# GpSimd waits for its own row transfers before every ninth one, in the sort and in the message steps of a graph network

## What is computed

```python
h = relu(layernorm(x))
edge_mats = (edge_attr @ W_bond + b_bond).reshape(-1, 32, 32)      # one 32x32 matrix an edge
for _ in range(4):                                                 # four message steps
    msg = einsum('eij,ej->ei', edge_mats, h[dst])                  # row gather by edge
    agg = segment_sum(msg, src, num_segments=12500)                # sum by the other end
    h = gru_cell(agg, h, ...)
x = x + h
h = relu(layernorm(x))
norm = deg_inv_sqrt[src] * edge_weight * deg_inv_sqrt[dst]
out = x + segment_sum(h[src] * norm[:, None], dst, 12500)
```

## Time and profile before

| | us |
|---|---|
| Time, median of 3 runs | 32566.4 (32561.8 to 32571.98) |
| Profiled execution, its own time | 32329.01 |
| Its span, first to last instruction | 32327.5 |
| Before the sort's scatters | 577.2 |
| Sort, first to last scatter | 6128.5 |
| Steps, first to last gather | 20044.9 |
| After the last gather | 5490.0 |
| GpSimd busy | 19193.7 (59%) |
| PE matmul busy | 18113.4 (56%) |
| DVE busy | 12316.8 (38%) |

### The profile page before, as it was taken

One profiled execution on the slowest core, in us unless ns is written; L12 is line 12 of the kernel. 1 busy time (PEld: TensorE's weight loads), 2 busy tenths in 40 slices (PEclk: granted clock), 3 DMA queues, 4 the chain that ended last, 5 costly groups with the idle time before them and its releaser, 6 DMA issues. The chain is left out here.

```text
span 32327.5 us, 272049 instructions
## 1 busy us (share of the span) xinstructions
PE 18113.4 (56%) x73252; PEld 11303.4 (35%) x73253; DVE 12316.8 (38%) x18995; ACT 6342.0 (20%) x11838; POOL 19193.7 (59%) x19883
## 2 busy tenths in 40 slices
PE   5444444447777757777767777775777773000004
PEld 4222222224444434444434444443444442000003
DVE  7555555533333333333333333333333333111113
ACT  4222222212222212222212222221222221000000
POOL 2444444466666656666656666665666665777772
PEclk5666666678888878888878888887888886555555
DMA  2222222211111111111111111111111111222224
GB/s 87 81 77 77 81 77 77 81 35 29 29 29 29 29 25 29 29 29 28 29 26 27 29 29 29 30 28 25 29 29 30 30 29 36 55 55 55 55 55 123
DMA packets 2423090, 1449.76 MB, mean 45 GB/s; under 512 B 1772221, under 2 KB 2253002, under 8 KB 2404167
## 3 DMA queue, kind: packets, MB, share of 16 engines
q1 hardware_dynamic: 720484, 980.18, 10.0%
q0 software_dynamic: 635936, 335.84, 6.4%
q10 hardware_dynamic: 1066560, 132.51, 2.7%
HBM read 1035.83 MB, written 411.12 MB: 45 GB/s over the span
## 5 line engine op out<-in xcount | busy, mean ns | idle before, releaser
L1112 POOL DMA_INDIRECT h_rows<-h_table,rec x12928 | 12195.4, 943 | 7353.8 <-issue 3880.5
L1298 PE MATMUL outer<-a_masked,h_by_quarter 128*128 128x272 f32 x25856 | 8240.2, 447 | 5227.6 <-DVE h_by_quarter L1158 2359.8
L1298 PEld LDWEIGHTS outer<-a_masked,h_by_quarter 128*128 128x128 f32 x25856 | 5378.2, 216 | 9576.1 <-issue 7355.3
L1266 PE MATMUL msg_psum<-outer_sums,w_bond_blocks 128*128 128x512 f32 x13736 | 7718.0, 652 | 0.0
L1344 ACT COPY outer_sums<-outer 128x544 f32<-128x544 f32 x6464 | 3900.2, 613 | 15272.9 <-PE outer L1298 7098.1
L865 POOL DMA_INDIRECT edges_by_node<-row,place x3125 | 2992.3, 958 | 3188.2 <-DVE row L792 2273.2
L1598 POOL DMA_INDIRECT messages_by_bucket<-ms,ix x3232 | 3418.9, 1058 | 1149.1 <-issue 1124.9
L1150 DVE TENSOR_TENSOR a_masked<-rec,gates 128x4352 f32<-128x4352 f32 x808 | 3782.5, 4681 | 53.1 <-PE outer L1298 31.5
L1266 PEld LDWEIGHTS msg_psum<-outer_sums,w_bond_blocks 128*128 128x128 f32 x13736 | 2921.0, 213 | 923.6 <-issue 260.9
L1167 DVE TENSOR_TENSOR_SCAN scan<-carry_flags,scan,msg_psum 128x512 f32<-128x512 f32 x404 | 517.1, 1280 | 6706.2 <-PE msg_psum L1266 4495.5
L1158 DVE TENSOR_TENSOR h_by_quarter<-h_rows,gates 128x2048 f32<-128x2048 f32 x808 | 1846.0, 2285 | 1824.4 <-DMA h_rows<-h_table,rec 1786.2
(11 more groups left out here) (273 smaller groups left out, 12928.5 us busy)
## 6 DMA issues: line engine op xcount, KB each, us to landing
h_rows<-h_table,rec POOLq DMA_INDIRECT x12928
key_row<-source_keys SPq DMA_DIRECT2D x125, 1600.0 KB
rec<-edges_by_node SPq DMA_DIRECT2D x1010, 168.0 KB
carry_flags<-carry_flags SPq DMA_DIRECT2D x505, 256.0 KB
chunk_sums<-scan_t ACTq DMA_DIRECT2D x1616, 64.0 KB
low_key_row<-source_low_keys SPq DMA_DIRECT2D x126, 800.0 KB
mr<-messages_by_bucket SPq DMA_DIRECT2D x220, 392.0 KB, 3.0
messages_by_bucket<-zeros SPq DMA_DIRECT2D x125, 689.5 KB
```

Source lines behind the costliest of these rows:

```text
L1112: pool.indirect_dma_start(out=hb[r][:, u, :], out_offset=None, in_=ht, in_offset=bass.IndirectOffsetOnAxis(ap=rec[r][:, u, W_DST:W_DST + 1 ...
L1266: last = pe.matmul(pm[:, 0:GW], wb[:, k, :], ts[b][:, k, :], start=(k == 0), stop=(k == K1 - 1))
L1298: last = pe.matmul(pt[g % RING][:, u, 0:KC], hq[j][:, g * GPB + u, :, :].rearrange("p q d -> p (q d)"), am[j][:, g * GPB + u, :, :].rearra ...
```

## The change

In the sort, GpSimd stops in front of scatters 8 and 16 (counted from 0) of each iteration until all earlier scatters of that iteration have landed. In the steps, it stops in front of gather 0 of a tile until the 16 gathers of the tile before have landed, and in front of gather 8 until gathers 0 to 7 have. Its wait for PE in front of gather 10 goes; the one in front of gather 0 stays. Nothing is computed otherwise.

```diff
@@ scatter, sort
                         for u in range(J1):
+                            if u in (8, 16):
+                                pool.wait_ge(s_sc[b], i * (16 * J1) + 16 * u)
+                                hold(pool)
                             pool.indirect_dma_start(
@@ steps
-            LATER = HALF + 2
@@ group, steps, GpSimd
                                 for u in range(J3):
-                                    if u in (0, LATER) and past:
-                                        pool.wait_ge(s_t, n0 * NB + (j * NB + NB + (HALF // GPB if u else 0)))
+                                    if u == 0 and past:
+                                        pool.wait_ge(s_t, n0 * NB + (j * NB + NB))
+                                        hold(pool)
+                                    if u == 0 and (j or past):
+                                        other = b * GI if j else (1 - b) * GI + GI - 1
+                                        pool.wait_ge(s_hg[other], (s * USES[b if j else 1 - b] + i) * (16 * J3) + (16 * J3 if j or b else 0))
+                                        hold(pool)
+                                    if u == HALF:
+                                        pool.wait_ge(s_hg[r], (s * USES[b] + i) * (16 * J3) + 16 * u)
                                         hold(pool)
                                     pool.indirect_dma_start(
```

## The result

The changed kernel takes 31,719.7 us (median of 4 runs, 31,685 to 31,774) against 32,569.2 us before (4 runs), a ratio of 0.974 with a 95% interval of 0.9724 to 0.9757. Predicted were 31,145 us. It lies in the range and on the forecast side, but 575 us above the forecast, and close to rival A's 31,770 us. Its profiled execution took 31,727.1 us, in the midst of the others: there is no gap between profile and median like the 237 us of before.

The account below looks back on a forecast made before the run. Late PE signals behind unbroken runs of about nine or more indirect DMAs bound sort and steps. Profiled 32,329 - 1500 (sort) + 80 (steps) = 30,909 us; with 237 us from profile to median, 31,145 us. Range 30,700 to 31,950 us.

Parts of the forecast that it names:

- rival A: Sort: the run of 17 scatters stays, most iterations take 42 us; 875 us gained, 80 lost, 31,770 us; chance 0.12.
- The bound: Sort and steps: unbroken runs of about nine or more indirect DMAs delay PE's signals until GpSimd pauses.
- A stop's cost: GpSimd's gap at a stop: 2.25 us for gathers, 2.15 for scatters, in place of 0.30; bounds 1.5 and above 3.68.
- Sort, GpSimd's floor of 35.6 us: Sort: GpSimd's scatters 31.6 us, two stops adding 3.7, passage to the next iteration 0.3: 35.6 us an iteration.
- Sort, 37.0 us an iteration: Sort: mean iteration 37.0 us instead of 49.0, gaining 1500 us over 125 iterations; bounds 35.6 and 41 us.
- the alternation: Sort: a run of 17 scatters makes iterations alternate between 35.6 us and 36 to 42 us.
- Steps, 23.94 us a tile: Steps: GpSimd's tile with two stops takes 23.94 us against 23.84, +80 us; bounds -320 to +640 us.
- the slack: Steps: PE is done at 43.3 us, gather 0 of tile n+2 is due at 47.8: 4.5 us of slack.
- The sum: Whole kernel: 32329 - 1500 + 80 = 30909 us profiled; with the 237 us between profile and median, 31,145 us, 4.4% less.
- B: Rival: lateness follows the number of DMAs, stops clear nothing; sort +460 us, steps +2600 us, together 35,600 us; chance 0.09.
- C: Rival: a stop of 2.0 us and a sort at GpSimd's floor; 1675 + 320 us gained, 30,570 us; chance 0.06.
- D: Rival: nothing happens in sort and steps, as the waits might be met when reached; the prediction rejected it.

## Why the prediction was right, and where it was off

*The bound* was read rightly. Late signals of PE beside unbroken runs hold back the sort; breaking the runs gives 1190 us.

*A stop's cost:* 2.15 us for a scatter against 1.97 us measured, 2.25 for a gather against 2.2. The two parts put together were right where nothing else moves data.

*Sort, GpSimd's floor of 35.6 us:* right. It is seen as 35.3 us with pauses by work.

*Sort, 37.0 us an iteration:* this term is 3.0 us too low, 375 us. The step that failed is that PE's signals "start to be late about 10 us after the run of scatters began, at its ninth": runs of eight and nine were taken as free, and only one of 17 as harmful. In the changed kernel the run of nine delays by 7.5 us a signal that PE gave 5.45 us after the run began, and a run of eight delays by 5.9 us one given after 4.1 us; the two runs of eight carry 1450 of the 2288 us of lateness. The trace of before had it already: of 79 results that PE finished during a run's sixth row, 56 were copied over 1 us late. So no iteration is free, GpSimd hardly ever gets ahead, only one run of 17 forms, and the alternation does not come. Where it came, with pauses by work, its long iteration was 57 us, not 42.

*Steps, 23.94 us a tile:* 0.52 us too low, 420 us (the forecast of +80 us became +330 against a usual execution of the old steps). The term that was mis-sized is the stop, taken at 2.25 us everywhere. In front of the second tile of a group it is 3.09 us, where the landing meets the load of `carry_flags`; in front of a first tile it is 2.19 and in front of gather 8 it is 2.20. That makes (3.09 + 2.19) / 2 + 2.20 = 4.84 us a tile instead of 4.50. The other 0.18 us stand in front of gather 1: its gap is 0.53 us in the mean, 0.23 over the usual 0.30, and not the 0.05 that was added for it. That a wait for a landing can also wait for what moves beside it was missing. The rest held: GpSimd hardly waits for PE (5.5 us in all), the slack was there, and the wait in front of gather 10 is worth nothing.

*The sum.* Carrying over the 237 us between profile and runs was wrong in kind. They lay in the two stages that the change touches, and the changed kernel's profile and median agree within 8 us. So the miss is made of three parts: 375 us in the sort, 420 in the steps, less the 237 that were added without reason, is 558 of 575 us; the stretch behind the last gather is 20 us longer than before. That the 237 us went the right way is luck: without them the miss would have been over 800 us.

*The signs.* Two of the prediction's own signs of being wrong came: gaps of 3 us and more, and late signals within runs of eight. ACT's "remote" waits for `next_free` were to fall under 1000 us and fell to 2284.7, and GpSimd's idle time in front of a first scatter was to be often under 1 us and was 5.4. In the steps most of the signs came, the stops of 2.2 us in part. So the time came near by a part of the mechanism, not by all of it.

*The rivals.* A's time came out, by another mechanism and other terms: only one run of 17 stays, iterations take 40.0 us and not 42, and the steps lose 330 us and not 80. B, that a stop clears nothing, was wrong for stops of 2 us, and right for a pause of 1.1 us, where the steps lost even more than B had it (27.85 us a tile against 27.1). Its "stops of more than 3.0 us" happened too, but only at 139 of the 804 stops in front of a gather 0. C and D fell. The rule of the Trainium skill named in the prediction, to wait for a DMA late ("DMA: Bandwidth & Descriptors", Rules for kernel authors), agrees with the steps: the waits laid open cost 330 us there. In the sort breaking the run was worth more.

## What to carry to other kernels

When waits are marked "remote" and end within about 2 us of the end of a run of GpSimd's indirect DMAs, try breaking the run before looking at the sender. Here breaks of about 2 us after every eight were enough in the steps, where breaks of 1.1 us did not help, and took away about a quarter of the sort's late waits. The break need not be a wait: GpSimd's own work does as well, and where a bulk load of another queue meets the landing it is the shorter of the two. And where the profiled execution and the median differ by more than the runs do among themselves, find the stage that varies before adding the difference to a forecast.

## What the runs showed that was not expected

- A pause in the steps must be about 2 us long: 1.11 us gave 27.85 us a tile, 1.69 us 24.32, 2.19 us 24.02. Late signals come 1.87 and 1.91 us after the last row's end in two places shown, 2.85 us in the earlier trace rows and 0.22 us in a run of eight; one shown comes while its run still goes on.
- How long a run may be has no one answer. In the steps runs of eight leave 6.7 us of late copies, with runs of eleven it is 2046.8 us. In the sort runs of eight and nine leave 2284.7 us, and late ones begin with a run's third row, while at the end of a run of 13 signals pass at once. Why the two stages differ is open.
- A gather's rows are with DVE 1.45 us after the end of GpSimd's row, and 4.85 us after it when a load of 256 KB was issued 1.55 us before that end.
- The same code differs between groups of runs by more than within one: the kernel before has medians from 32,316.8 to 32,722.8 us in five groups, of which four are on record as run on four different chips, and the sort with three pauses by work took 4896, 4930, 4964 and 4652 us. The last is 37.2 us an iteration, GpSimd's own bound. Why signals were prompter there is open.
